# A recommendation tower whose GpSimd delays the second tile's gathers until the first x1 is cast

## The reference

```
e  = stack([tbl_f[ids[:, f]] for f in range(39)], axis=1)            # (1024, 39, 16)
x1 = relu(einsum('bhd,bmd,shm->bsd', e,  e, W1) + b1)                 # (1024, 128, 16)
x2 = relu(einsum('bhd,bmd,shm->bsd', x1, e, W2) + b2)                 # (1024, 128, 16)
z  = concatenate([x1.sum(-1), x2.sum(-1)], axis=-1)                   # (1024, 256)
h  = relu(concatenate([z, dense_ctx], 1) @ W_top1 + b_top1)           # 512
h  = relu(h @ W_top2 + b_top2)                                        # 256
y  = h @ W_top3                                                       # (1024, 1)
```

## Time and profile before

| what | value |
|---|---|
| median of three timed runs | 1201.86 us |
| profiled execution, its own time | 1213.87 us |
| its span, from first to last instruction | 1212.1 us |
| TensorE busy | 1121.3 us (93%) |
| VectorE busy | 947.1 us (78%) |
| GpSimd busy | 847.6 us (70%) |
| ScalarE busy | 798.4 us (66%) |
| mean granted clock of TensorE | 0.992 of full speed |
| moved by the DMA engines | 154.47 MB, mean 127 GB/s |

### The profile page before, as it was taken

How to read it: one execution, slowest core, us unless ns; L and a number is a source line. 1 busy time by engine, 2 the same in 40 slices (tenths; PEclk the granted TensorE clock), 3 DMA queues, 4 the chain that set the end, 5 groups by cost and what they waited for, 6 DMA issues and landing times.

```text
span 1212.1 us, 17500 instructions
## 1 busy us (share of the span) xinstructions
PE 1121.3 (93%) x4468; PEld 827.8 (68%) x4468; DVE 947.1 (78%) x2846; ACT 798.4 (66%) x2718; POOL 847.6 (70%) x956
## 2 busy tenths in 40 slices
PE   0059999999999999999999999999999999999996
PEld 0037777777777777777776567777777777776684
DVE  2027889899898889888898468998888988875786
ACT  4016767777777777767776467777676777765683
POOL 7744887778678878778778456788777864542455
PEclk9999999999999999999999999999999999999998
DMA  5246568675876477665976238764686749662341
GB/s 168 46 122 134 109 128 181 132 150 98 182 163 127 94 149 176 140 124 109 194 137 142 45 70 181 170 130 92 135 178 125 146 97 202 146 135 44 71 93 33
DMA packets 73516, 154.47 MB, mean 127 GB/s; under 512 B 14339, under 2 KB 27525, under 8 KB 73414
## 3 DMA queue, kind: packets, MB, share of 16 engines
q0 software_dynamic: 28272, 85.81, 39.4%
q1 hardware_dynamic: 45142, 67.53, 20.7%
HBM read 66.26 MB, written 3.81 MB: 58 GB/s over the span
## 4 chain that ended last, share of the span: by engine, by line
PE 45%; POOL 20%; issue 15%; DMA 11%; DVE 6%; ACT 2%; another core or an unknown queue 1%; SPq 0%; POOLq 0%; DVEq 0%; ACTq 0%
PE bank L605 35%; DMA prod<-prod 10%; PE l_acc L589 8%; POOL tree L307 6%; POOL emb L278 5%; POOL tree L314 3%; POOL prod L289 3%; DVE acc L507 2%; POOL tree L319 2%; POOL a_sum L328 2%; PE misc L625 1%; DVE t_sum L516 1%; DMA prod<-w_by_h 1%; ACT prod L395 1%
## 5 line engine op out<-in xcount | busy, mean ns | idle before, releaser
L395 ACT ACTIVATE prod<-bank,emb 128x128 f32<-128x128 f32 x2560 | 721.9, 375 | 329.5 <-PE bank L605 297.4
L507 DVE SCALAR_TENSOR_TENSOR acc<-bank,emb,acc 128x128 f32<-128x128 f32 x2176 | 611.9, 342 | 149.1 <-PE bank L605 134.1
L605 PE MATMUL bank<-w2h,x1h 128*128 128x512 f32 (+1 forms) x1280 | 540.5, 422 | 13.5 <-DVE acc L507 9.7
L605 PE MATMUL bank<-w2l,x1h 128*128 128x512 f32 (+1 forms) x1280 | 495.6, 387 | 0.0
L605 PE MATMUL bank<-w2h,x1l 128*128 128x512 f32 (+1 forms) x1280 | 471.2, 430 | 2.7 <-issue 1.5
L278 POOL DMA_INDIRECT emb<-tbl,idx x312 | 309.7, 993 | 82.3 <-issue 75.9
L605 PEld LDWEIGHTS bank<-w2h,x1h 128*128 128x128 f32 x1280 | 241.4, 189 | 120.2 <-issue 59.8
L605 PEld LDWEIGHTS bank<-w2h,x1l 128*128 128x128 f32 x1280 | 241.1, 188 | 90.6 <-issue 37.0
L307 POOL TENSOR_TENSOR tree<-prod 128x640 f32<-128x640 f32 x128 | 240.9, 1882 | 86.1 <-DMA prod<-prod 86.0
L605 PEld LDWEIGHTS bank<-w2l,x1h 128*128 128x128 f32 x1280 | 241.4, 189 | 62.8 <-issue 23.3
L289 POOL DMA_DIRECT2D prod<-prod x127 | 124.8, 982 | 185.7 <-ACT prod L395 182.7
(11 more groups left out here) (79 smaller groups left out, 278.5 us busy)
## 6 DMA issues: line engine op xcount, KB each, us to landing
prod<-prod POOLq DMA_DIRECT2D x127, 640.0 KB
z<-e_rows SPq DMA_DIRECT2D x160, 234.0 KB
z<-e_rows SPq DMA_DIRECT2D x192, 78.0 KB
emb<-tbl,idx POOLq DMA_INDIRECT x312
z<-e_rows SPq DMA_DIRECT2D x32, 156.0 KB
prod<-w_by_h SPq DMA_DIRECT2D x3, 832.0 KB
e_rows<-e_t SPq DMA_DIRECT2D x8, 256.0 KB
wt<-w_top SPq DMA_DIRECT2D x2, 512.0 KB
```

What stands on the lines that cost most here:

```text
L395: last = nc.scalar.activation(prod[:, ct % P_RING, i, n * S:(n + 1) * S], bank[:, (ct * NB + k) % RING, n * S:(n + 1) * S], ACT.Copy, scal ...
L507: nc.vector.scalar_tensor_tensor(dst, src, scale, dst if step else b2_row[:, :], ALU.mult, ALU.add).then_inc(v_step, 1)
L605: last = nc.tensor.matmul(out_bank[:, 0:b - a], x, w[:, a:b], start=(n == 0), stop=(n == 2))
```

## The change

Two edits. GpSimd waits, ahead of the 40th gather (the first of tile 1), for `x1h_done`, which ScalarE raises when x1 of chunk 0 is cast. And the number of gathers issued ahead of column tile ct is capped at 8 + 4 ct.

```
+FIRST_GATHERS = 8

         def gathers_before(ct):
-            return min((TILES - 1) * M, -(-M * (ct + 9) // 16))
+            return min((TILES - 1) * M, -(-M * (ct + 9) // 16), FIRST_GATHERS + 4 * ct)

                 if f == 0 and tile == 1:
                     pool.wait_ge(in_idx, 16)
+                    pool.wait_ge(x1h_done, 1)
```

## The result

| | before | after |
|---|---|---|
| median, us | 1202.12 (1199.68 to 1203.82, 7 runs) | 1209.44 (1207.30 to 1214.83, 7 runs) |
| profiled execution, us (span) | 1213.87 (1212.1) | 1209.10 (1207.3) |

The seven runs of the kernel before are the three of the table ahead of the prediction and four more. The ratio after to before is 1.0072, interval 1.0055 to 1.0090: by it the change costs 8.7 us (6.6 to 10.8), by the medians 7.3, where 6.3 was forecast. The profiled executions say the opposite, since that of before holds the opening stall.

The account below looks back on a forecast made before the run. After the opening TensorE was taken to be full, so each microsecond it stands still lengthens the result. Merge 1.4 + late lift 4.2 + clock 1.7 - opening 1.0 = +6.3 on 1201.86 gave 1208.2 us, range 1195 to 1212 (8 in 10).

Parts of the forecast that it names:

- GpSimd falls behind by 8.0: Column tiles 3 to 7: four gathers make 9.2 us per tile where 8.3 is allowed; ct 7's transfer 8.0 us late.
- Point 1: VectorE's merge of chunk 0 waits 2.1 us for a_sum of ct 3; TensorE loses 1.4 (ends 0 and 2.1).
- Point 2: ScalarE gets the adder of ct 5, needed for ct 8, 2.2 us late; cost 0 (ends 0 and 2.2).
- Point 3: Second tile's late lift, chunk 2 step 15: TensorE waits 4.2 us for the 39th gather (ends 0 and 6.5).
- Point 4: The merge of chunk 1 needs ct 9's round at 186.9 against its turn at 186.6; cost 0.3, left out.
- Point 5: Behind the lift's 4.2 us wait TensorE's clock falls to half speed, costing 1.7 us (ends 0 and 3.4).
- The opening, -1.0: With gathers moved away from the z loads, layer 2 starts 1.0 us earlier (ends 0 and 2.2).
- belong to that execution alone: The 12.0 us between profiled and timed runs are about the opening's stall, taken as peculiar to that one profiled execution.
- The faster rival: The 10.7 us opening stall belongs to the kernel and fewer early DMAs dissolve it: -4.4 to -7.8, 1194 us; chance 0.22.
- two odd records: In the opening: ScalarE copies e_rep at 71.54 before its load's issues end at 72.99; VectorE released at 88.45 by nothing traced.

Follow-up runs that it names:

- the kernel with seven gathers ahead of ct 7: The changed kernel with 39 instead of 36 gathers issued ahead of ct 7, so one remains ahead of ct 8; chip A: 1207.94 us, ratio 1.0040.
- Ramp without the wait: The changed kernel's cap of 8 + 4 ct, without the wait for x1h; chip A: 1209.92 us, ratio 1.0062 to the kernel before.
- four first gathers: The changed kernel with FIRST_GATHERS 4 instead of 8; chip C: 1218.73 us, ratio 1.0054 to the kernel before.
- the place without the lag: The kernel before, no wait, with gathers ahead of ct 6 to 9 set to 36, 36, 40, 44; chip B: 1202.19 us, ratio 0.9995.
- the lag at the lift alone: The kernel before, no wait, with gathers ahead of ct 7 and 8 held at 38, so the 39th goes ahead of ct 9; chip C: 1218.93 us, ratio 1.0044.
- the late lift five steps later: The changed kernel with the late lift at step 20 instead of 15 and its copy at 22 instead of 17; chip C: 1227.91 us, ratio 1.0120.
- The pause for z: Against the kernel before: GpSimd waits for chunk 0's second z load group, then issues 16, 22, 27 gathers, old schedule after; chip B: 1203.26 us, ratio 1.0003.
- second profile of before: The kernel before, unchanged, profiled again on chip A: 1202.18 us, ratio 1.0000; profile span 1201.5, without the opening stall.
- twelve first gathers: The changed kernel with FIRST_GATHERS 12 instead of 8; chip B: 1208.30 us, ratio 1.0050 to the kernel before.
- the kernel with the wait and no ramp: The changed kernel's wait for x1h with the old gather counts, 22 ahead of ct 0; chip B: 1212.48 us, ratio 1.0079 to the kernel before.

## Why the prediction was right, and where it was wrong

Forecast was 1.4 + 4.2 + 1.7 - 1.0 = +6.3. The profile has 1.0 + 4.3 + 2.9 for the three losses, 8.2 before any gain in the opening, and the timed runs 6.6 to 10.8. The mechanism is the one that was forecast.

- **GpSimd falls behind by 8.0.** Right: 8.4, at 9.1 to 9.6 per tile with four gathers (forecast 9.2). By the prediction's own pitch its three steps of 9.2 end at 164.0 and the lag at 8.1, not 163.9 and 8.0, which changes nothing.
- **Point 1, the merge.** Right: VectorE waits 2.29 (forecast 2.1). TensorE's own wait is 1.02 (forecast 1.4), and chunk 1 as a whole is 2.1 longer.
- **Point 2, ScalarE, at 0.** Right in the changed kernel. It was the next to bind: in the kernel with seven gathers ahead of ct 7 it does.
- **Point 3, the late lift.** Right: 4.31 (forecast 4.2). Ramp without the wait: 4.10; four first gathers: 9.36; the place without the lag: none; the lag at the lift alone: 3.70 and +5.3 us. The wait follows the lateness of the 39th gather.
- **Point 4, the second merge, left out.** Right: no wait there. It waits 4.02 where the lift does not (the late lift five steps later).
- **Point 5, the clock.** The mis-sized term: put at 1.7, it measured 2.9 (5.89 us of matmuls in a stretch of 6.83 at 0.50). The forecast took the shorter of the two stretches it had seen. It varies between profiles: 3.02 us of matmuls at 0.50 in the ramp without the wait, 4.46 in the changed kernel on chip C, 5.92 with the lag at the lift alone, so 1.5 to 3.0 by the same halving.
- **The opening, -1.0.** Not seen in the timed runs. Layer 2 starts at 74.5 to 76.7 in the eight profiles with the wait for x1h (mean 75.7), and at 76.4 to 78.0 in the five in which the gathers run on (mean 77.3): 1.6 sooner, with ranges that overlap. In the changed kernel's profile the half clock in 75.35:78.76 takes 1.6 back; such a stretch right behind layer 2's start is in four of the eight profiles with the wait and in two of the five without. The ratios of the ramp with the wait (1.0072) and without it (1.0062) don't tell the gain from none.
- **The step that failed** is the claim that the 12.0 us of the profiled stall "belong to that execution alone". By the runs they belong to a chip. On chip C all 28 runs of the kernel before take 1210 to 1220; the kernel with only the late gathers moved (1218.93) shows VectorE's 10.03 "remote" there, and a chunk 0 of 43.0 us. From chunk 8 to the end it takes 857.5, as the kernels on the other chips do, so what chip C adds lies in the opening. With gathers held back on the same chip chunk 0 is 34.6 (four first gathers), 35.7 (lift later) and 37.3 (the changed kernel); in the last two a shorter idle of VectorE is left (4.06 and 5.22). The faster rival, priced at -4.4, is thus true on that chip: -2.9. The forecast was added to the median of timed runs, none of them above 1203.82 and so not from a chip like C (none of 28 below 1210). That the runs of the result came from chips without the stall too was luck, as far as the prediction could know. Beside the size of the difference the argument for "one execution" had two odd records, and it never asked whether another chip makes one. A sign was in the trace, which the forecast did not use; SyncE's queue in the first profile of before:

```profile
56.44 11.65 SPq L246 DMA_DIRECT2D z<-e_rows  x9
```

Left open: what in chip C makes SyncE's issues slow beside gathers (one profile there, and the first of before), and why the stall outlasts the gathers (up to 79.0) by 9.5 us. Slow issues are not the whole of it: layer 2 starts at 78.05 with them on chip C and at 78.04 without them in the ramp without the wait on chip A, and the shorter stall has none. No profile of the unchanged kernel was taken on chip C. That the first profile of before came from such a chip is likely by the rows that it shares with the late-gathers kernel (11.65 and 11.29, 10.72 and 10.03), not shown. The pause for z was not tried on chip C; it could remove the stall there without the lag.

## What to carry to other kernels

Work that runs into idle time is free, and the same work inside a loop whose other engine is full is not: count instructions times pitch against the period (4 x 1.3 + 4 against 8.3 here), add up the lag, and ask of each consumer in order of time whether its slack is larger. A lag fixed at one consumer moves to the next, so put the ramp right rather than one deadline. When a profiled time and the timed ones differ by 1%, look for another chip as well as for another execution, before choosing which of them a forecast is for.

## What the hardware did that was not expected

- **VectorE's merges beside GpSimd's adders.** The 128x512 merges between SBUF tiles take 0.67 us alone; in the second profile of before the 25 that overlap a 128x640 adder take 1.78 on average, the 66 others 0.67 (the eight that only apply the relu, line 524, not counted); in the kernel with twelve first gathers two took 3.57 and 3.61. The Trainium skill, page SBUF — State Buffer, section SBUF: two separate sides, says that VectorE and GpSimd take turns at a shared port pair, each keeping it for a whole instruction; the rows of the kernel with twelve first gathers agree in that merge and adder do not proceed together (3.57 against 0.68). They do not fit the section's further statement that whichever starts first gets the pair: by the recorded starts both merges began about 1 us ahead of the adder (165.77 against 166.76, 174.03 against 175.09) and still ended only 0.56 behind it. GpSimd was in a gather at both starts, but 39 first merges that started in a gather with another gather behind it took 0.68, over all fourteen profiles. Spans on GpSimd are rough; why the merge is held before the adder's recorded start stays open.
- **The clock after an idle.** Stretches at 0.50 were 3.4 us behind idles of 4.10 and 3.63 and 6.8 behind idles of 4.31, 4.33, 3.70 and 3.01; 10.2 behind 9.36; 13.7 behind 11.12; 3.4 behind 2.59, 2.42, 1.94 and 1.90, none behind 2.41. The same idle of 2.19 ahead of layer 2 was followed by a stretch of 3.4 in four profiles of twelve. The length of the idle alone thus does not tell. Half of TensorE's busy time in the stretch is what it costs: 1.5 to 3.1 on top of a wait of 3 to 4.3 us.
- **An accumulating transfer beside loads.** It lands in 5.6 us in the median of the whole run (row below, last column; DMA issues after) and takes 11.1 from its start to its adder in the kernel with the wait and no ramp, where z loads, gathers and another such transfer run beside it. The row is of that kernel.

```profile
prod<-prod POOLq DMA_DIRECT2D x127, 640.0 KB, 5.6
```

- **Chips differ.** The same kernel takes 1202 on two chips and 1213 on a third. By the kernel with only the late gathers moved, the difference is one stall in the opening, and the order of DMAs lengthens and shortens it.
